# A two-layer conditioned transformer on one core: the first norm's scale and the first two projections of layer 0 interleaved by chunks of 128 features, with the loads in that order and three small inputs in one array

## The chip, the cores and the metric

The kernel runs on 1 core of one Trainium2 chip. The metric is the device time of one execution in microseconds (us). Kernel code is written per engine: TensorE (PE), VectorE (DVE), ScalarE (ACT), GpSimd (POOL) and SyncE (SP), which here only issues transfers. Each engine runs its own list of instructions in order; engines wait for each other and for transfers through semaphores.

## The reference, cut to what matters

x is (32, 64, 512): 32 entries of 64 tokens, 2048 tokens in all. cond_2048 is (32, 512), one row of conditioning for each entry.

```python
def ada_rms(x, t, w, tw):
    n = x * jax.lax.rsqrt(jnp.mean(jnp.square(x), axis=-1, keepdims=True) + EPS)
    scale = t @ tw.T
    return n * (w * (1.0 + scale))[:, None, :]
...
# layer 0: 8 query heads of 64, one key and one value head
h = ada_rms(x, time_emb, ln1_w, ln1_tw)
q, k, v = h @ Wq.T, h @ Wk.T, h @ Wv.T          # reshaped to heads
q, k = apply_rope(q, pos_ids), apply_rope(k, pos_ids)
attn = softmax(q k^T / sqrt(64)); x = x + (attn v) @ Wo.T
h = ada_rms(x, time_emb, ln2_w, ln2_tw)
x = x + (silu(h @ Wg.T) * (h @ Wu.T)) @ Wd.T     # inner size 2048
# layer 1: layernorm with scale and shift t @ W_ada.T + b_ada, latent keys and values,
# 16 query heads of 32, rope, softmax under a mask, output projection, residual
```

## The kernel before

The tokens are cut into 16 tiles of 128 (NT = 16; P = 128), so a tile holds two entries. Features are cut into four chunks of 128 (KT = 4). Layer 0's attention runs tile by tile, its MLP in blocks of 512 tokens, layer 1's attention tile by tile again; the MLP's matmuls are laid between the attention pieces of later tiles by numbers written out by hand (`FILL0`, `FILL1`). The order on each engine is the order of the code. This study concerns the first 30 us, in which nothing of the MLP is there yet.

**The scale of the first norm.** `condt` holds the conditioning turned (features on partitions, NB = 32 entries along the columns). For each chunk k of the contraction, `condition(k, ...)` issues four matmuls, one for each group g of 128 output features. The stationary operand is the same 128x32 piece of `condt`; each goes to a column tile of the array of its own (`tile_position=(0, NB * g)`) and so to its own 32 partitions of the bank BU. When all four chunks have been added up, ACT copies the 128x128 result to `tq` (`condition_copy`), PE turns it (`condition_T`), DVE forms (1 + scale) * w for all 512 features at once (`adaptive_scale(0, ...)`, L1255), and `scale_h(t)` multiplies the turned tile `xt[t]` of x by it (L1294, 128x512).

**The first two projections.** Tiles 0 and 1 are projected in full fp32: `first_qkv(t)` (L783) runs for each chunk k two matmuls of 320 columns (`QK0`; queries, keys and values are 640), with `xt[t][:, k]` stationary and `wst[:, k]` moving. Tile 2 and later ones use weights split into a high and a low part (`wqh`, `wql`): ACT rounds `wst[:, k]` to `wqh` (`split_qkv`, L1793), DVE subtracts it (`split_qkv`, L1262, 128x640, both inputs in SBUF). A tile is split in the same way: `high_h` on ACT, `low_h` on POOL (L563).

**After a projection.** `rope_mul(t)` on DVE (L1344, twice 128x640 out of PSUM, then two small ones for the keys, L1353 and L1354), `rope_sum(t)` on POOL (L574, L575), `qk_T(t)` on PE (L816, L817, five transposes), `keys(t)` on DVE (L1359) and `queries(t)` on ACT, then `scores(t)` on PE (L834). The rms factor of a tile comes from `square(t)` on ACT, `mean_sq(t)` on DVE and `rstd(t)` on POOL (L544, L552) and is folded into the rope tables `cs0`, for which `rope_mul(t)` waits. DVE also computes the angles of the rope (L1219 to L1248) at the start.

**Warming.** `keep_warm(n)` (L775) issues n matmuls of zeros with 256 columns into a bank that nobody reads.

**Loads.** SP issues them in the order in which they are written: `condt`, four chunks of `adaw0` (the weights of the first scale, ln1_tw turned, cut along the contraction), `xt[0]`, four chunks of `wst`, then `xres[0]`, `xt[1]` and the rest. ACT issues the small ones (`posi`, `invt`, `idn`, `lnw` twice).

## Time and profile before

| | us |
|---|---|
| median of 3 runs | 836.48 (835.95 to 837.05) |
| the profiled execution | 836.44 |
| its span in the trace | 834.6 |
| PE busy | 827.2 (99%) |
| DVE busy | 598.5 (72%) |
| ACT busy | 414.1 (50%) |
| POOL busy | 392.4 (47%) |

The span runs from the first to the last instruction in the trace; the 1.8 us more of the execution's own time lie around it. A busy PE is one that has an instruction in flight: matmuls overlap, and a record's length holds the way through the array as well. An fp32 matmul that is not a transpose leaves two records. Every time in the rows below counts from the start of the span.

### The profile page before, as it was taken

The page shows a single profiled execution, that of the slowest core. Times are in us where ns is not written, and L with a number is a line of the kernel's source. Part 1 is how long each engine was busy: PE and PEld are TensorE (multiplying, and loading weights), DVE is VectorE, ACT ScalarE, POOL GpSimd, SP SyncE. Part 2 cuts the span into 40 slices and gives each one's busy share as a digit, 9 for nine tenths or more (in the row PEclk, how much of TensorE's full clock was granted, in tenths as well). Part 3 has the DMA queues.
Part 4 walks back from the last instruction along what each step waited for, and adds up shares of the span by engine and source line. Part 5 has one row for each costly group of instructions (what it writes and reads, how often), then busy time and mean ns, then how long its engine had stood idle before and what let it go on. Part 6 is the DMA issues. An engine that isn't in the chain of part 4 may idle for free.

```text
span 834.6 us, 15041 instructions
## 1 busy us (share of the span) xinstructions
PE 827.2 (99%) x5688; PEld 678.6 (81%) x5688; DVE 598.5 (72%) x889; ACT 414.1 (50%) x725; POOL 392.4 (47%) x310
## 2 busy tenths in 40 slices
PE   9999999999999999999999999999999999999998
PEld 5888878888788788787888887888878878878886
DVE  6986567666665766766656878877867668678997
ACT  4555445435345344345446475373453543735662
POOL 2667535545544446446545755454443533532110
PEclk9999999999999999999999999999999999999999
DMA  9913442433523523424444445355254353330001
GB/s 334 387 34 110 137 158 98 162 119 116 175 101 104 183 92 131 158 68 154 145 154 143 144 166 196 115 177 169 83 184 155 105 196 124 124 132 14 15 27 52
DMA packets 73335, 113.50 MB, mean 136 GB/s; under 512 B 6320, under 2 KB 39088, under 8 KB 73264
## 3 DMA queue, kind: packets, MB, share of 16 engines
q1 hardware_dynamic: 72544, 112.45, 39.8%
q8 instruction: 46, 0.75, 0.4%
q14 instruction: 25, 0.20, 0.1%
q10 hardware_dynamic: 720, 0.09, 0.1%
HBM read 88.15 MB, written 24.38 MB: 135 GB/s over the span
## 4 chain that ended last, share of the span: by engine, by line
PE 95%; DVE 2%; DMA 1%; issue 1%; ACT 0%; POOL 0%; SPq 0%; ACTq 0%; DVEq 0%; POOLq 0%
PE ps L736 29%; PE ps L738 28%; PE ps L737 28%; PE ps L1024 2%; PE ps L834 1%; PE ps L1052 1%; PE ps L783 1%; DMA pT<-turned_p 1%; PE ps L864 1%; PE ps L775 1%; DVE ex L1529 1%; PE ps L1032 1%; PE ps L745 1%; PE ps L992 0%; DMA turned_p<-tp 0%
## 5 line engine op out<-in xcount | busy, mean ns | idle before, releaser
L736 PE MATMUL ps<-h2h,guh 128*128 128x512 f32 x512 | 203.5, 397 | 0.0
L738 PE MATMUL ps<-h2l,guh 128*128 128x512 f32 x512 | 199.9, 391 | 0.0
L737 PE MATMUL ps<-h2h,gul 128*128 128x512 f32 x512 | 199.3, 389 | 0.0
L590 POOL TENSOR_TENSOR gul<-rgu,guh 128x1024 fp32r<-128x1024 f32 x64 | 161.0, 2516 | 71.2 <-ACT guh L1890 71.2
L595 POOL TENSOR_TENSOR wdl<-rwd,wdh 128x512 fp32r<-128x512 f32 x64 | 83.5, 1304 | 129.4 <-ACT wdh L1898 129.4
L1415 DVE TENSOR_TENSOR xres<-ps,xres 128x512 f32<-128x512 f32 x128 | 87.4, 684 | 62.7 <-PE ps L738 62.7
L736 PEld LDWEIGHTS ps<-h2h,guh 128*128 128x128 f32 x512 | 96.0, 188 | 27.4 <-issue 7.7
L738 PEld LDWEIGHTS ps<-h2l,guh 128*128 128x128 f32 x512 | 96.1, 188 | 21.2
L737 PEld LDWEIGHTS ps<-h2h,gul 128*128 128x128 f32 x512 | 96.2, 188 | 19.1
L736 PE MATMUL ps<-wdh,ah 128*128 128x512 f32 x256 | 100.1, 391 | 0.0
L737 PE MATMUL ps<-wdh,al 128*128 128x512 f32 x256 | 99.6, 389 | 0.0
L738 PE MATMUL ps<-wdl,ah 128*128 128x512 f32 x256 | 99.6, 389 | 0.0
L1898 ACT CAST wdh<-rwd 128x512 fp32r<-128x512 f32 x64 | 39.4, 616 | 107.5 <-PE ps L738 104.3
L1410 DVE TENSOR_TENSOR al<-af,ah 128x512 fp32r<-128x512 f32 x64 | 64.7, 1011 | 36.8 <-ACT ah L1909 36.3
L1405 DVE TENSOR_TENSOR af<-ps,sg 128x512 f32<-128x512 f32 x64 | 44.0, 688 | 64.4 <-PE ps L738 46.6
L1909 ACT CAST ah<-af 128x512 fp32r<-128x512 f32 x64 | 39.6, 618 | 87.9 <-DVE af L1405 87.9
L1903 ACT ACTIVATE sg<-ps 128x512 f32<-128x512 f32 x64 | 38.2, 596 | 89.7 <-PE ps L738 89.5
L1890 ACT CAST guh<-rgu 128x1024 fp32r<-128x1024 f32 x64 | 67.0, 1046 | 0.0
L736 PEld LDWEIGHTS ps<-wdh,ah 128*128 128x128 f32 x256 | 48.0, 188 | 10.9 <-DVE al L1410 1.0
L738 PEld LDWEIGHTS ps<-wdl,ah 128*128 128x128 f32 x256 | 48.0, 188 | 10.1
L737 PEld LDWEIGHTS ps<-wdh,al 128*128 128x128 f32 x256 | 48.1, 188 | 9.8
L627 POOL TENSOR_TENSOR yl<-yf,yh 128x512 fp32r<-128x512 f32 x16 | 20.6, 1290 | 56.4 <-ACT yh L1988 56.4
(199 smaller groups left out, 1588.1 us busy)
## 6 DMA issues: line engine op xcount, KB each, us to landing
rgu<-gu SPq DMA_DIRECT2D x64, 512.0 KB, 4.7
rwd<-WdT SPq DMA_DIRECT2D x64, 256.0 KB, 4.2
turned_q<-tq SPq DMA_DIRECT2D x20, 320.0 KB, 3.0
qkT<-turned_q SPq DMA_DIRECT2D x20, 320.0 KB, 3.2
turned_p<-tp SPq DMA_DIRECT2D x9, 512.0 KB, 2.6
pT<-turned_p SPq DMA_DIRECT2D x9, 512.0 KB, 4.0
xt<-xT SPq DMA_DIRECT2D x15, 256.0 KB, 2.9
out<-xres SPq DMA_DIRECT2D x15, 256.0 KB, 3.5
```

Of the source, the lines that this page charges most:

```text
L590: pool.tensor_tensor(gul[i][:, :], rgu[i][:, :], guh[i][:, :], ALU.subtract).then_inc(m_gul, 1)
L595: pool.tensor_tensor(wdl[r][:, :], rwd[n % 2][:, :], wdh[r][:, :], ALU.subtract).then_inc(m_wdl, 1)
L736: pe.matmul(dst, lh, rh, start=start, stop=False)
L737: pe.matmul(dst, ll, rh, start=False, stop=False)
L738: return pe.matmul(dst, lh, rl, start=False, stop=stop)
L1405: dve.tensor_tensor(af[:, :], bank(BU), sg[:, :], ALU.mult).then_inc(m_af, 1)
L1410: dve.tensor_tensor(al[n % RING][:, :], af[:, :], ah[n % RING][:, :], ALU.subtract).then_inc(m_al, 1)
L1415: dve.tensor_tensor(at, bank(down_bank(q, i)), at, ALU.add).then_inc(m_x, 1)
L1890: act.copy(guh[i][:, :], rgu[i][:, :]).then_inc(m_guh, 1)
L1898: act.copy(wdh[r][:, :], rwd[n % 2][:, :]).then_inc(m_wdh, 1)
L1903: act.activation(sg[:, :], bank(BG), ACT.Silu).then_inc(m_sg, 1)
L1909: act.copy(ah[n % RING][:, :], af[:, :]).then_inc(m_ah, 1)
```

## The change

Four things are changed together.

1. **The first scale goes by groups of output features.** `first_scale(g)` computes the scale of the 128 features of group g completely: four matmuls, one for each chunk k of the contraction, all four to the same column tile (0, NB * g). ACT copies 32x128 of it (`first_scale_copy`), `first_scale_T(g)` turns it, DVE's `first_scale(g)` forms (1 + scale) * w for that group and `scale_part(t, g)` multiplies that chunk of `xt[t]` (128x128). For this, ln1_tw comes from the host in another layout, so that a chunk of `adaw0` holds one group of outputs with the whole contraction.
2. **The projections of tiles 0 and 1 are cut by chunk**, `first_qkv(t, k)`, and laid between the pieces of the scale. The transposes of tile 0 come after both, with half of the second norm's scale (`condition_second`) ahead of them and half behind. One `keep_warm(1)` stands between the first scale's matmuls and its transpose; the three between the chunks are gone.
3. **The loads follow**: `condt`, then `adaw0` chunk, `wst` chunk, and so on, with both `xt` ahead; the loads of `adaw1`, `adaw2` and `xres[3:6]` are cut into pieces with semaphores of their own.
4. **The identity, the two norm weights and the inverse frequencies come in one array** `small` (tile `consts`, 128x168), in one transfer in place of four; `condT` comes with 512 contiguous bytes to a partition.

DVE, ACT and POOL have their early work in another order, too: on DVE, angle steps, `first_scale`, `scale_part` and `split_qkv` are interleaved, and on POOL `rope_sum(0)` comes ahead of `low_h(2)`.

The diff, cut to its core (POOL's part is word for word the three lines of its reordering):

```diff
-            sp.dma_start(condt[:, :, :], by_row(condT)).then_inc(ld_cond, 16)
-            for k in range(KT):
-                sp.dma_start(adaw0[:, k, :], by_row(ln1_twT)[:, k, :]).then_inc(ld_ln1[k], 16)
-            load_xT(0)
-            for k in range(KT):
-                sp.dma_start(wst[:, k, :], by_row(WqkvT)[:, k, :]).then_inc(ld_qkv[k], 16)
-            sp.dma_start(xres[:, 0, :], xv[:, 0, :]).then_inc(ld_x0, 16)
-            load_xT(1)
+            sp.dma_start(condt[:, :, :], condT).then_inc(ld_cond, 16)
+            for g in range(KT):
+                sp.dma_start(adaw0[:, g, :], ln1_tw[g, :, :]).then_inc(ld_ln1[g], 16)
+                if g == 0:
+                    load_xT(0)
+                if g == KT - 1:
+                    sp.dma_start(xres[:, 0, :], xv[:, 0, :]).then_inc(ld_x0, 16)
+                sp.dma_start(wst[:, g, :], by_row(WqkvT)[:, g, :]).then_inc(ld_qkv[g], 16)
+                if g == 0:
+                    load_xT(1)
             sp.dma_start(xres[:, 1, :], xv[:, 1, :]).then_inc(ld_x1, 16)
             sp.dma_start(gf[:, :, :], xT[2, :, :, :]).then_inc(ld_x2t, 16)
-            sp.dma_start(adaw1[:, :, :], by_row(ln2_twT)).then_inc(ld_ln2, 16)
+            for k in range(KT):
+                sp.dma_start(adaw1[:, k, :], by_row(ln2_twT)[:, k, :]).then_inc(ld_ln2[k], 16)
             sp.dma_start(xres[:, 2, :], xv[:, 2, :]).then_inc(ld_x2, 16)
             sp.dma_start(wost[:, :, :], by_row(WoT)).then_inc(ld_wo, 16)
-            sp.dma_start(adaw2[:, :, :], by_row(adaT)).then_inc(ld_ada, 16)
+            for i, ks in enumerate((slice(0, 1), slice(1, KT))):
+                sp.dma_start(adaw2[:, ks, :], by_row(adaT)[:, ks, :]).then_inc(ld_ada[i], 16)
+            sp.dma_start(xres[:, 3, :], xv[:, 3, :]).then_inc(ld_x3, 16)
             load_xT(3)
-            sp.dma_start(xres[:, 3:6, :], xv[:, 3:6, :]).then_inc(ld_x3, 16)
+            sp.dma_start(xres[:, 4:6, :], xv[:, 4:6, :]).then_inc(ld_x4, 16)
...
             rstd(1)
+            rope_sum(0)
             low_h(2)
-            rope_sum(0)
+            rope_sum(1)
             rstd(2)
-            rope_sum(1)
...
+            def first_scale(g):
+                pe.wait_ge(ld_ln1[g], 16)
+                rows = slice(NB * g, NB * (g + 1))
+                for k in range(KT):
+                    mm = pe.matmul(ps[rows, first_bank(g), 0:P], condt[:, k, :], adaw0[:, g, P * k:P * (k + 1)],
+                                   start=(k == 0), stop=(k == KT - 1), tile_position=(0, NB * g))
+                mm.then_inc(first_mm, 1)
+
+            def first_scale_T(g):
+                pe.wait_ge(first_sb, g + 1)
+                rows = slice(NB * g, NB * (g + 1))
+                pe.transpose(ps[:, first_bank(g), P:P + NB], tq[rows, 0:P], idn[rows, rows],
+                             tile_position=(NB * g, 0)).then_inc(first_T, 1)
...
+            def first_qkv(t, k, between=None):
+
+                pe.wait_ge(a_xs[t], k + 1)
+                pe.wait_ge(ld_qkv[k], 16)
+                for c in range(2):
+                    mm = pe.matmul(ps[:, qkv_banks(t)[c], 0:QK0], xt[t][:, k, :],
+                                   wst[:, k, QK0 * c:QK0 * (c + 1)],
+                                   start=(k == 0), stop=(k == KT - 1))
+                    if c == 0 and between is not None:
+                        between()
+                if k == KT - 1:
+                    mm.then_inc(a_qkv, 1)
...
             pe.wait_ge(ld_cond, 16)
-            for k in range(KT):
-                pe.wait_ge(ld_ln1[k], 16)
-                mm = condition(k, in_blocks(adaw0, k))
-                if k < KT - 1:
-                    keep_warm(1)
-            mm.then_inc(ada_mm, 1)
-            pe.wait_ge(ld_idn, 16)
-            condition_T(1, 1, BD[0])
+            first_scale(0)
+            keep_warm(1)
+            pe.wait_ge(ld_const, 16)
+            first_scale_T(0)
             keep_warm(3)
-            first_qkv(0)
-            first_qkv(1)
+            first_qkv(0, 0)
+            first_scale(1)
+            first_qkv(1, 0, lambda: first_scale_T(1))
+            first_scale(2)
+            first_qkv(0, 1)
+            first_scale_T(2)
+            first_scale(3)
+            first_qkv(1, 1)
+            first_scale_T(3)
+            first_qkv(0, 2)
+            first_qkv(0, 3)
+            first_qkv(1, 2)
+            first_qkv(1, 3)
+            condition_second((0, 1))
             qk_T(0)
-            condition_second()
+            condition_second((2, 3))
             scores(0)
-            condition_T(2, 1, BG)
+            condition_T(1, 1, BG)
...
+            def first_scale(g):
+                dve.wait_ge(first_T, g + 1)
+                dve.scalar_tensor_tensor(out=sc_ln1[:, g, :], in0=ps[:, first_bank(g), P:P + NB], scalar=1.0,
+                                         in1=lnw[:, 0, g:g + 1].broadcast_to([P, NB]),
+                                         op0=ALU.add, op1=ALU.mult).then_inc(first_done, 1)
+
+            def scale_part(t, k):
+                dve.wait_ge(first_done, k + 1)
+                if k == 0:
+                    dve.wait_ge(ld_xt[t], 16)
+                h = xt[t][:, k, :].rearrange("p (b s) -> p b s", b=2)
+                dve.tensor_tensor(h, h, sc_ln1[:, k, 2 * t:2 * t + 2].unsqueeze(2).broadcast_to([P, 2, S]),
+                                  ALU.mult).then_inc(a_xs[t], 1)
+
...
-            adaptive_scale(0, sc_ln1, BD[0])
-            scale_h(0)
-            angles_end()
+            first_scale(2)
+            scale_part(0, 2)
+            scale_part(1, 2)
             split_qkv(0)
+            first_scale(3)
+            scale_part(0, 3)
+            mean_sq(0)
+            scale_part(1, 3)
             split_qkv(1)
-            mean_sq(0)
-            scale_h(1)
+            scale_h(2)
+            mean_sq(1)
+            rope_mul(0)
             split_qkv(2)
-            mean_sq(1)
-            scale_h(2)
-            rope_mul(0)
             split_qkv(3)
-            mean_sq(2)
             keys(0)
             rope_mul(1, lambda: softmax_sub(0))
+            mean_sq(2)
...
+            def first_scale_copy(g):
+                act.wait_ge(first_mm, g + 1)
+                rows = slice(NB * g, NB * (g + 1))
+                act.copy(tq[rows, 0:P], ps[rows, first_bank(g), 0:P]).then_inc(first_sb, 1)
...
-            condition_copy(1, 1)
+            first_scale_copy(0)
             split_qkv(0)
+            first_scale_copy(1)
+            split_qkv(1)
+            first_scale_copy(2)
+            split_qkv(2)
             rope_table(0)
-            split_qkv(1)
+            first_scale_copy(3)
             rope_table(1)
             square(0)
-            split_qkv(2)
             split_qkv(3)
             square(1)
             high_h(2)
-            square(2)
             values(0)
             act.activation(spare_exp[:, :], minus_half[:, :], ACT.Exp)
             queries(0)
-            condition_copy(2, 1)
+            condition_copy(1, 1)
+            square(2)
```

What moves on PE, at the start of the program. Before:

```order
L775 MATMUL ps<-zeros 128x256 x4
L745 MATMUL ps<-adaw,condt 32x128 x4
L775 MATMUL ps<-zeros 128x256
L745 MATMUL ps<-adaw,condt 32x128 x4
L775 MATMUL ps<-zeros 128x256
L745 MATMUL ps<-adaw,condt 32x128 x4
L775 MATMUL ps<-zeros 128x256
L745 MATMUL ps<-adaw,condt 32x128 x4
L755 MATMUL ps<-idn,tq 128x128
L775 MATMUL ps<-zeros 128x256 x3
L783 MATMUL ps<-wst,xt 128x320 x16
L816 MATMUL ps<-idn,qr 128x128 x4
```

And in the changed kernel (L804 is `keep_warm`, L770 `first_scale`, L777 `first_scale_T`, L811 `first_qkv`):

```order
L804 MATMUL ps<-zeros 128x256
L777 MATMUL ps<-consts,tq 128x32
L804 MATMUL ps<-zeros 128x256 x3
L811 MATMUL ps<-wst,xt 128x320 x2
L770 MATMUL ps<-adaw,condt 32x128 x4
L811 MATMUL ps<-wst,xt 128x320
L777 MATMUL ps<-consts,tq 128x32
L811 MATMUL ps<-wst,xt 128x320
L770 MATMUL ps<-adaw,condt 32x128 x4
L811 MATMUL ps<-wst,xt 128x320 x2
```

The 16 matmuls of the two projections stood in one piece behind the whole scale; now the first of them stand behind one quarter of it, and three quarters of the scale and three small transposes stand among them. The last eight of the 16 (chunks 2 and 3 of tile 0, then of tile 1) are in one piece again.

What moves on DVE, from the last scaling to the keys of tile 0. Before:

```order
L1262 TENSOR_TENSOR wql<-wst,wqh 128x640
L1280 TENSOR_SCALAR stat<-stat 128x1
L1294 TENSOR_TENSOR gf<-gf,sc_ln 128x512
L1344 TENSOR_TENSOR t<-ps,cs 128x640 x2
L1353 TENSOR_TENSOR qr<-t 128x2x32
L1354 TENSOR_TENSOR qr<-t 128x2x32
L1262 TENSOR_TENSOR wql<-wst,wqh 128x640
```

And in the changed kernel (L1321 is `split_qkv`, L1353 `scale_h`, L1403 to L1413 `rope_mul`, L1418 `keys`):

```order
L1321 TENSOR_TENSOR wql<-wst,wqh 128x640
L1353 TENSOR_TENSOR gf<-gf,sc_ln 128x512
L1339 TENSOR_SCALAR stat<-stat 128x1
L1403 TENSOR_TENSOR t<-ps,cs 128x640 x2
L1412 TENSOR_TENSOR qr<-t 128x2x32
L1413 TENSOR_TENSOR qr<-t 128x2x32
L1321 TENSOR_TENSOR wql<-wst,wqh 128x640 x2
L1418 COPY qkT<-ps 128x4x32
```

Between the rope of tile 0 and its keys stands one more of the four splits of the weights than before.

What moves on POOL, around the rope of tile 0. Before:

```order
L552 TENSOR_TENSOR cs<-cs,stat 128x64
L563 TENSOR_TENSOR hl<-gf,hh 128x512
L574 TENSOR_TENSOR qr<-t 128x8x32
L575 TENSOR_TENSOR qr<-t 128x8x32
L544 TENSOR_TENSOR stat<-stat,minus_half 128x1
```

And in the changed kernel (L588 and L589 are `rope_sum`, L577 `low_h`):

```order
L566 TENSOR_TENSOR cs<-cs,stat 128x64
L588 TENSOR_TENSOR qr<-t 128x8x32
L589 TENSOR_TENSOR qr<-t 128x8x32
L577 TENSOR_TENSOR hl<-gf,hh 128x512
L588 TENSOR_TENSOR qr<-t 128x8x32
```

The low part of tile 2 went from ahead of the rope of tile 0 to behind it.

## Rows read from the trace of the kernel before

**Rows 1.** The page: busy time of PE, and the chain that ended last.

```profile
PE 827.2 (99%) x5688; PEld 678.6 (81%) x5688; DVE 598.5 (72%) x889; ACT 414.1 (50%) x725; POOL 392.4 (47%) x310
...
PE 95%; DVE 2%; DMA 1%; issue 1%; ACT 0%; POOL 0%; SPq 0%; ACTq 0%; DVEq 0%; POOLq 0%
```

**Rows 2.** The chain in order of time: start us, us, what.

```profile
1.10 3.78 PE ps L775 x8
4.88 0.59 PE ps L745 x8
...
8.22 0.63 PE ps L775 x2
...
9.28 0.28 ACT tq L1798
...
9.99 1.30 PE ps L775 x6
11.29 8.77 PE ps L783 x32
20.05 0.62 PE ps L816 x4
...
20.78 1.01 PE ps L745 x32
21.79 0.62 PE ps L834 x32
22.41 0.26 PE ps L755
...
24.44 0.58 PE ps L816 x4
```

**Rows 3.** Timeline of DVE: start us, us, line, operation, tiles.

```profile
10.10 0.29 DVE L1255 SCALAR_TENSOR_TENSOR sc_ln<-ps,lnw 128x128 f32<-128x128 f32 x1 [1.24 <-PE ps L755]
...
12.56 1.55 DVE L1262 TENSOR_TENSOR wql<-wst,wqh 128x640 fp32r<-128x640 f32 x2
...
18.59 0.76 DVE L1354 TENSOR_TENSOR qr<-t 128x64 f32<-128x64 f32 x1
19.28 1.36 DVE L1262 TENSOR_TENSOR wql<-wst,wqh 128x640 fp32r<-128x640 f32 x1
...
20.82 0.29 DVE L1359 COPY qkT<-ps 128x128 f32<-128x128 f32 x1
21.02 1.55 DVE L1344 TENSOR_TENSOR t<-ps,cs 128x640 f32<-128x640 f32 x2
...
24.08 0.21 DVE L1354 TENSOR_TENSOR qr<-t 128x64 f32<-128x64 f32 x1
```

**Rows 4.** Timeline of POOL: start us, us, line, operation, tiles.

```profile
17.31 1.28 POOL L563 TENSOR_TENSOR hl<-gf,hh 128x512 fp32r<-128x512 f32 x1
18.54 0.74 POOL L574 TENSOR_TENSOR qr<-t 128x256 f32<-128x256 f32 x1
19.23 0.73 POOL L575 TENSOR_TENSOR qr<-t 128x256 f32<-128x256 f32 x1
...
22.65 0.74 POOL L574 TENSOR_TENSOR qr<-t 128x256 f32<-128x256 f32 x1 [0.94 <-DVE t L1344]
```

**Rows 5.** Stretches: us, busy of each engine, granted clock, DMA share, GB/s.

```profile
0.00:5.00 5.00, 3.90 (x12) 2.71 (x16) 0.14 (x1) 1.49 (x2) 0.55 (x6) 1.00 0.57 155
5.00:10.00 5.00, 4.52 (x40) 2.00 (x35) 3.66 (x7) 0.72 (x2) 0.00 (x0) 1.00 1.05 381
```

**Rows 6.** DMA issues (KB, us to landing) and the issue queues' timeline.

```profile
idn<-ident ACTq DMA_DIRECT2D x1, 64.0 KB, 4.1
wost<-WoT SPq DMA_DIRECT2D x1, 1024.0 KB, 11.4
...
8.78 0.46 SPq L459 DMA_DIRECT2D wost<-WoT  x1
```

More of the change, by code:

```diff
@@ L46, in fill, with build @@
         next(pieces, None)
-def build(nc, x, xT, pos, condT, ln1_w, ln1_twT, ln2_w, ln2_twT, WqkvT, WoT, gu, WdT,
-          adaT, b_ada, Wq1T, Wkd, wkvuT, Wo1T, invf, rope1, ident, out):
+def build(nc, x, xT, pos, condT, ln1_tw, ln2_twT, WqkvT, WoT, gu, WdT,
+          adaT, b_ada, Wq1T, Wkd, wkvuT, Wo1T, rope1, small, out):
     D = WoT.shape[0]
@@ L152, in build @@
             posi, posf = sb("posi", [P, NT], I32, l0), sb("posf", [P, NT], into=l0)
-            invt = sb("invt", [P, HD0 // 2], into=l0)
             sq = sb("sq", [P, D], into=l0)
@@ L165, in build @@
         smx1 = sb("smx1", [P, 3, 4 * KT])
-        (ld_pos, ld_cond, ld_lnw, ld_bada, ld_x0, ld_x1, ld_x2, ld_x2t, ld_idn, ld_wo, ld_x3, ld_x6, ld_ln2, ld_ada, ld_rope1,
-         ld_w1) = [sem("ld_" + n) for n in "pos cond lnw bada x0 x1 x2 x2t idn wo x3 x6 ln2 ada rope1 w1".split()]
+        (ld_pos, ld_cond, ld_const, ld_bada, ld_x0, ld_x1, ld_x2, ld_x2t, ld_wo, ld_x3, ld_x4, ld_x6, ld_rope1,
+         ld_w1) = [sem("ld_" + n) for n in "pos cond const bada x0 x1 x2 x2t wo x3 x4 x6 rope1 w1".split()]
         ld_ln1 = [sem(f"ld_ln1_{m}") for m in range(KT)]
+        ld_ln2 = [sem(f"ld_ln2_{m}") for m in range(KT)]
+        ld_ada = [sem(f"ld_ada_{m}") for m in range(2)]
+        first_mm, first_sb, first_T, first_done = [sem("first_" + n) for n in "mm sb T done".split()]
+        a_xs = [sem(f"a_xs{i}") for i in range(2)]
         ld_qkv = [sem(f"ld_qkv{k}") for k in range(KT)]
@@ L775, in keep_warm @@
                     pe.matmul(ps[:, BD[1], 0:2 * P], zeros[:, 0:P], zeros[:, :], start=True, stop=True)
-            def first_qkv(t):
-                pe.wait_ge(a_hf, t + 1)
-                for k in range(KT):
-                    pe.wait_ge(ld_qkv[k], 16)
-                    for c in range(2):
-                        mm = pe.matmul(ps[:, qkv_banks(t)[c], 0:QK0], xt[t][:, k, :],
-                                       wst[:, k, QK0 * c:QK0 * (c + 1)],
-                                       start=(k == 0), stop=(k == KT - 1))
-                mm.then_inc(a_qkv, 1)
+            def first_qkv(t, k, between=None):
[7 more added lines that the diff above has]
+                        between()
+                if k == KT - 1:
+                    mm.then_inc(a_qkv, 1)
             def qkv(t, between=None):
@@ L804, in qkv @@
                     for k in range(KT):
+                        if t == 2 and c == 0:
+                            pe.wait_ge(w0l, k + 1)
                         mm = three(ps[:, XB[c], 0:QK0], hh[:, k, :], hl[:, k, :], wqh[:, k, cols],
@@ L1228, in _ @@
             dve.tensor_scalar(turns, angle, 1.0 / TWO_PI, ROUND, ALU.mult, ALU.add).then_inc(ang_step, 1)
+            first_scale(0)
+            scale_part(0, 0)
             dve.wait_ge(ang_step, 3)
@@ L1238, in _ @@
                 step += 1
[L1240 to L1248 removed]
+                if part == C1:
+                    scale_part(1, 0)
+                if part == C2:
+                    first_scale(1)
+                    scale_part(0, 1)
+                    scale_part(1, 1)
+            dve.wait_ge(ang_step, step)
+            dve.tensor_scalar(red, red, float(np.float32(3.1415925)), -float(np.float32(3.1415925)),
+                              ALU.min, ALU.max).then_inc(ang_ready, 1)
+            dve.wait_ge(ang_ready, 1)
+            dve.scalar_tensor_tensor(out=angle, in0=red, scalar=-1.0, in1=red, op0=ALU.mult,
+                                     op1=ALU.max).then_inc(ang_step, 1)
+            dve.wait_ge(ang_step, step + 1)
+            dve.tensor_scalar(angle, angle, -1.0, float(np.pi / 2), ALU.mult, ALU.add).then_inc(ang_ready, 1)
             def adaptive_scale(n, tab, from_bank):
[L1251 to L1253 removed]
+                dve.wait_ge(ada_T, n)
                 by_block = ps[:, from_bank, 0:P].rearrange("p (k b) -> p k b", k=KT)
@@ L2068, in _ @@
             square(3)
[L2069 removed]
+            condition_copy(2, 2)
             for s in range(1, NT):
@@ L2199 @@
         "pos": turn(np.asarray(pos_BxS).reshape(B * T // 128, 128)),
-        "condT": turn(cond_2048),
-        "ln1_w": column(L0_cond_ln1_w), "ln1_twT": turn(L0_cond_ln1_tw),
-        "ln2_w": column(L0_cond_ln2_w), "ln2_twT": turn(L0_cond_ln2_tw),
+        "condT": np.ascontiguousarray(np.asarray(cond_2048).reshape(-1, D // 128, 128).transpose(2, 1, 0)),
+        "ln1_tw": np.ascontiguousarray(groups(L0_cond_ln1_tw).reshape(D // 128, 128, -1)), "ln2_twT": turn(L0_cond_ln2_tw),
         "WqkvT": turn(wqkv), "WoT": turn(L0_cond_Wo),
@@ L2207 @@
         "wkvuT": turn(kvu.reshape(-1, kvu.shape[-1])), "Wo1T": turn(wo1),
-        "invf": np.ascontiguousarray(np.broadcast_to(invf, (128, hd0 // 2))),
         "rope1": np.ascontiguousarray(np.concatenate([rope1] * (128 // T), 0)),
-        "ident": np.eye(128, dtype=f32),
+        "small": np.concatenate([np.eye(128, dtype=f32), column(L0_cond_ln1_w), column(L0_cond_ln2_w),
+                                 np.broadcast_to(invf, (128, hd0 // 2))], 1),
     }
```

69 lines of the change are left out of this document (30 added, 39 removed).

## The prediction

> **What bounds the kernel now.** First the page: PE is busy for 827.2 us, 99% of the span, and the chain that ended last lies on PE for 95% [rows 1]. So PE's list is the clock of the kernel: what comes later on PE near the start pushes everything behind it by as much, and nothing later has spare time to give it back. Then the chain in order of time for the part that is changed [rows 2]. The reader is to see three stretches. From 4.88 to 11.29 the first scale is formed: PE's four small pieces of work have warming matmuls between them (one pair takes 0.63), ACT's copy takes 0.28, and from 9.99 to 11.29 there are zeros only, while DVE makes the factor (0.29) and scales the tile [rows 2, 3]. From 11.29 to 20.05 run the projections of tiles 0 and 1, 8.77 without a gap. From 20.05 PE goes on without a gap through tile 0's transposes, the second norm's scale and, at 21.79, the scores. The 6.4 us before the projections are what the change can win, and it can win only PE time that holds nothing but zeros.
>
> **Step 1, the projections start earlier.** The loads allow it. By 10.00 the trace has moved 5 x 155 + 5 x 381 = 2680 KB [rows 5]. The first projection needs `condt`, one chunk of `adaw0`, `xt[0]` and one chunk of `wst`, 0.9 MB, which passes at about 5.3; chunk 1 of both weights is complete at 1.8 MB, about 7.7, and wanted at about 11 and 12. No later load binds: bytes and rate stay the same. The small array is issued second on ACT's queue; the identity took 4.1 from its issue [rows 6], so it is there by about 5.5, before 7.2.
> PE: the four matmuls of `first_scale(0)` go to one column tile. A warming record of 256 columns takes 3.78 / 8 = 0.47 at first and 1.30 / 6 = 0.217 later [rows 2], so PE works at the lower of its two levels (1.2 and 2.4 GHz) at first although the row of the stretch prints 1.00 [rows 5]. A record of 128 columns is half of that, 0.22 and 0.108. Eight records: 4.88 + 8 x 0.22 = 6.65. ACT's copy (0.28 and 0.1 around it) and the warming matmul lie side by side to about 7.2, the small transpose and three warming matmuls (0.3 and 1.30) follow to **8.8**. DVE's two small operations (each under the 0.29 of the whole factor) lie beside them. The projections so start 2.5 earlier than at 11.29.
>
> **Step 2, three quarters of the scale now stand among them.** What do four matmuls of 128 columns cost in one column tile? Before, 16 of them, going round the four tiles, took 1.01 for 32 records [rows 2], 0.032 a record, against 0.108 for a record that has the array to itself. That is 0.25 for four at one end (if a chain in one tile overlapped as well), 8 x 0.108 = 0.87 at the other. I take 0.87: the ratio 0.108 / 0.032 is nearly the four tiles, so it is the tiles that ran side by side, and a chain that adds into one place in one tile has nothing beside it. To this comes the change between a narrow tile and the full array: 0.63 for the two warming records behind a narrow piece, where 0.43 is their bare time, so 0.2 a round. Three pieces: 3 x 1.07 = 3.2. Three small transposes, each 0.15 (a full one 0.26 with its neighbours' change): 0.45. The end of the projections: 8.8 + 8.77 + 3.2 + 0.45 = **21.2**, against 20.05, **1.15 later**. The early start is more than paid back.
> The Trainium skill, TensorEngine Tiling (Array Packing), Key Properties, says that changing the tiling mode drains the array. The 0.2 a round agrees that a change costs something; if each of the further changes cost a whole drain, the length of a record beyond its own 0.108, the sum would be up to 1 us larger, an estimate from that page's rule. TensorE: Matmul & The Clock Gate, Part 3 (Packing small matmuls), of the Trainium skill lets matmuls overlap when their tiles differ; no row here has a chain in one tile.
>
> **Step 3, tile 0's transposes lose their cover.** Before, tile 0's rope lay beside tile 1's projection and ended just as PE came free (POOL's second half ran 19.23 to 19.96, PE went on at 20.05) [rows 2, 4]. Now tile 0's last chunk ends four matmuls before the end, 21.2 - 4 x 0.548 = 19.0. DVE comes to the rope at about 19.3 (its factor, scalings and a split stand before it), takes 1.55, POOL starts 0.08 later (22.57 to 22.65) and takes 0.74 + 0.73 less 0.05 [rows 3, 4]: 22.35. So `qk_T(0)` starts at **22.35**, 2.3 later than before; the half of the second scale that now lies ahead of it (0.54) is work that it had to do anyway, and about 0.5 is PE waiting. `low_h(2)`, now behind, costs nothing there: its reader comes at 24.
>
> **Step 4, tile 0's keys.** PE could start the scores at 22.35 + 0.73 + 0.6 = 23.65. But `keys(0)` on DVE now stands behind two splits instead of one, and they meet POOL. A split takes 0.78 alone (1.55 for two at 12.56); at 19.28, beside POOL's sum, it took 1.36; the small rope operation took 0.76 beside POOL's sum and 0.21 with POOL quiet; both ended when POOL's operation had ended, plus their own time [rows 3, 4]. So a DVE operation with two inputs in SBUF waits for a POOL operation that runs. By this: the rope's small ones to 21.8, the first split behind POOL's second half, 22.35 + 0.7 = 23.1, then `low_h(2)` (1.28) takes its turn to 24.4, the second split to 25.1, keys to **25.4**. If POOL's long one comes behind both splits instead, keys are there at 24.0. The scores so start at 24.0 to 25.4 against 21.79; I take 25.0, nearer to the end that the rows at 19.28 show: 3.2 later. The Trainium skill, SBUF — State Buffer, in its part on the shared port pair, states the same hold for both directions, the later one blocking fully; by it POOL's `low_h` could also be the one held, which is the end at 24.0.
>
> **Step 5.** Tile 1's rope starts behind `keys(0)`, so 1.55, 0.08 and 1.42 later `qk_T(1)` can start at 28.4, when PE, 2.65 behind the start of the scores as before (21.79 to 24.44) [rows 2], comes at 27.7 to 28.1; before there was no such wait. 0.1 to 0.5, I take 0.2. SP's four more issues (0.46 each) delay none that matters: `wost` landed 11.4 after its issue at 8.78, being behind others' bytes and not its own issue [rows 6].
>
> **The sum**: 3.2 + 0.2 = **3.4 us later**. The profiled execution, 836.44, stands 0.04 under the median of 836.48, so the same sum holds for it: **839.8**. The likeliest case's own range is +1.7 to +4.6.
>
> **The rivals.**
> *Not slower: a chain in one tile costs what the round of four did.* Then step 2 costs 3 x 0.45 and `first_scale(0)` 0.6, the projections end at 8.2 + 8.77 + 1.35 + 0.45 = 18.8, `qk_T(0)` starts at 19.9 and the scores at 21.3 to 22.8, -0.5 to +1.1: **836.8**. For it speaks 0.032 a record in the row of 32; against it that this row has four tiles. It decides where a piece costs under 0.45 instead of 1.07. 20%, all of it within 0.2%.
> *Faster:* that case, and the waits behind it shrink too, since more is ready in advance. The 0.2% (1.7 us, about what a measurement of this kernel tells from no change) must come from PE's gaps before 35 us. 834.6. No row names such a gap as one that the change removes: 9%.
> *Slower by more:* each of the changes of tile drains the array and both splits wait in turn: 1 more in step 2 and 0.4 more in step 4, **841.3**. It decides where a round costs 0.4 instead of 0.2. 9%.
> *The change does not do what it says:* a chunk lands late and the projections wait for it. By step 1 there are 3 us to spare at chunk 1; inside the 62% of my forecast.
>
> **How the numbers follow.** Forecast 62%, slower by more 9%: 71% slower by over 0.2%. 20% within, 9% faster. The range takes in most of the "not slower" case and "slower by more": 836.3 to 841.6; it leaves out the 9% below, some 6% of the 20%, and some 4% above.
>
> **What would show it.** Right: the first projection starts near 8.8; the eight records of a `first_scale` amid the projections lie 0.11 apart; the projections end near 21.2; PE waits at `qk_T(0)` for POOL's sum and at `scores(0)` for DVE's keys; from there every line of PE stands 3 to 4 later to the end. Wrong: records 0.03 apart and an end before 20; or splits of 0.8 beside POOL's `low_h`, keys at 24, and a shift of 2 or less; or a late shift that shrinks after 30, which would say that PE's list has room behind the start.

## The result and the profile after

The changed kernel takes **841.69 us** in the median of 5 runs (841.14 to 842.86) against 836.48 (835.92 to 837.06) in 5 runs of the kernel before beside it: ratio 1.0066, 95% interval 1.0054 to 1.0077, 5.2 us slower. The forecast was 839.8 with a range to 841.6. The direction and most places were right, the size was 1.8 too small and the time lies just outside the range. The profiled execution took 841.43.

The page of the changed kernel answers to [rows 1]:

```profile
PE 831.5 (99%) x5687; PEld 682.2 (81%) x5687; DVE 602.2 (72%) x898; ACT 415.4 (49%) x728; POOL 392.3 (47%) x310
PE 89%; DVE 4%; DMA 3%; issue 2%; ACT 2%; POOL 1%; SPq 0%; DVEq 0%; ACTq 0%; POOLq 0%
```

PE is still busy for 99%, but the chain that ended last has left it for 11% of the span instead of 5%. The timeline of PE in the changed kernel answers to [rows 2] (start us, us, engine, line, operation, tiles, count, and the idle time before with what ended it):

```profile
4.54 1.03 PE L770 MATMUL ps<-adaw,condt 128*32 128x128 f32 x8
...
7.70 1.24 PE L811 MATMUL ps<-wst,xt 128*128 128x320 f32 x4
8.87 1.06 PE L770 MATMUL ps<-adaw,condt 128*32 128x128 f32 x8
9.86 0.81 PE L811 MATMUL ps<-wst,xt 128*128 128x320 f32 x2
10.60 0.24 PE L777 MATMUL ps<-consts,tq 32*128 32x32 f32 x1
10.77 0.81 PE L811 MATMUL ps<-wst,xt 128*128 128x320 f32 x2
11.51 1.06 PE L770 MATMUL ps<-adaw,condt 128*32 128x128 f32 x8
12.50 1.34 PE L811 MATMUL ps<-wst,xt 128*128 128x320 f32 x4
13.78 0.24 PE L777 MATMUL ps<-consts,tq 32*128 32x32 f32 x1
...
14.94 1.34 PE L811 MATMUL ps<-wst,xt 128*128 128x320 f32 x4
16.21 0.24 PE L777 MATMUL ps<-consts,tq 32*128 32x32 f32 x1
16.39 4.58 PE L811 MATMUL ps<-wst,xt 128*128 128x320 f32 x16
20.89 0.64 PE L759 MATMUL ps<-adaw,condt 128*32 128x128 f32 x16
22.03 0.66 PE L847 MATMUL ps<-consts,qr 128*128 128x128 f32 x4 [0.50 <-POOL qr L589]
...
24.83 1.13 PE L865 MATMUL ps<-qkT 64*64 64x64 f32 x32 [1.46 <-DVE qkT L1418]
...
28.75 0.60 PE L847 MATMUL ps<-consts,qr 128*128 128x128 f32 x4
...
31.06 0.60 PE L874 MATMUL ps<-consts,ex 128*128 128x128 f32 x4
```

The same view of the kernel before puts its starts up to 0.12 earlier than the chain of [rows 2] does, and the comparisons below use it (first projection, `scores(0)`, tile 1's transposes, `p_T(0)`; the projections end at 20.02):

```profile
11.17 8.88 PE L783 MATMUL ps<-wst,xt 128*128 128x320 f32 x32
...
21.72 0.69 PE L834 MATMUL ps<-qkT 64*64 64x64 f32 x32
...
24.39 0.63 PE L816 MATMUL ps<-idn,qr 128*128 128x128 f32 x4
...
26.73 0.60 PE L843 MATMUL ps<-idn,ex 128*128 128x128 f32 x4
```

The projections start at 7.70 (11.17 before) and end at 20.89 (20.02 before). A piece of scale takes 0.99 from its start to the next line's (8.87 to 9.86), a small transpose 0.17. Then PE waits 0.50 at tile 0's transposes and 1.46 at its scores. `p_T(0)`, the transposes of tile 0's probabilities (L874), is at 31.06; the first trace of the kernel before has it at 26.73, so the shift there is 4.3. It is 4.3 at `context(0)`, the product of tile 0's probabilities and values that follows, 4.1 at the last tile of layer 0 and 5.0 at the end.

DVE's timeline answers to [rows 3], POOL's to [rows 4]:

```profile
21.31 3.17 DVE L1321 TENSOR_TENSOR wql<-wst,wqh 128x640 fp32r<-128x640 f32 x2
24.40 0.28 DVE L1418 COPY qkT<-ps 128x128 f32<-128x128 f32 x1
...
29.12 1.61 DVE L1448 TENSOR_TENSOR ex<-ex,smx 128x512 f32<-128x512 f32 x1
```

```profile
21.94 1.86 POOL L577 TENSOR_TENSOR hl<-gf,hh 128x512 fp32r<-128x512 f32 x1
...
28.88 1.30 POOL L593 TENSOR_TENSOR wol<-wost,woh 128x512 fp32r<-128x512 f32 x1
```

Two splits ahead of tile 0's keys take 3.17 between POOL's sum and its low half for tile 2. And there is a second such place that the prediction did not name: `softmax_norm(0)` (L1448) takes 1.61 and ends 0.55 after `low_wo(0)` (L593, 28.88 to 30.18). In the kernel before `low_wo(0)` was nearly over when it began, and it took 0.69 (POOL's line, then DVE's):

```profile
24.37 1.29 POOL L579 TENSOR_TENSOR wol<-wost,woh 128x512 fp32r<-128x512 f32 x1 [0.29 <-DVE qr L1354]
...
25.56 0.69 DVE L1389 TENSOR_TENSOR ex<-ex,smx 128x512 f32<-128x512 f32 x1
```

The stretches of the changed kernel (columns as in [rows 5]) show loads at the same rate as before (377 GB/s from 5 to 10 us for 381), and a granted clock that fell:

```profile
20.00:25.00 5.00, 3.05 (x47) 1.85 (x49) 4.97 (x7) 3.89 (x8) 3.26 (x3) 0.96 1.02 399
25.00:30.00 5.00, 5.00 (x55) 4.87 (x55) 4.66 (x10) 2.70 (x5) 3.33 (x5) 0.70 1.06 378
```

Behind PE's two waits the granted clock was at its lower level (1.2 of 2.4 GHz) for 3.4 us; the scores took 1.13 (0.69 before). PE came to `p_T(0)` without a wait in this execution: its slow matmuls lay over the time in which the softmax was held.

### The profile page after: what moved, and what is told of

Its sections match the earlier page's. It is cut to its first block, busy times and chain, and to the rows that moved or that the text cites. A ratio compares the mean times of both kernels' runs of the same rounds, so it can differ in the third digit from the quotient of the medians.

```text
span 839.6 us, 15061 instructions
## 1 busy us (share of the span) xinstructions
PE 831.5 (99%) x5687; PEld 682.2 (81%) x5687; DVE 602.2 (72%) x898; ACT 415.4 (49%) x728; POOL 392.3 (47%) x310
## 4 chain that ended last, share of the span: by engine, by line
PE 89%; DVE 4%; DMA 3%; issue 2%; ACT 2%; POOL 1%; SPq 0%; DVEq 0%; ACTq 0%; POOLq 0%
PE ps L750 27%; PE ps L752 26%; PE ps L751 26%; PE ps L1055 1%; PE ps L865 1%; PE ps L1083 1%; PE ps L895 1%; DMA pT<-turned_p 1%; DVE ex L1588 1%; DMA turned_q<-tq 1%; PE ps L804 1%; POOL wol L662 1%; PE ps L1063 1%; PE ps L811 1%; PE ps L770 0%
```

## The experiments

Shifts below are against the first trace of the kernel before, where nothing else is said; every ratio is against runs of the kernel before on the same chip.

**Each kernel once more.** One trace of each was a thin basis, so both were profiled again, unchanged.

> The kernel before, unchanged, profiled once more. Theory (the shift that grows in layer 1 by 0.4 to 2.4 us between 455 and 720 us belongs to the single execution, not to the kernel): this second profile differs from the first by under 0.2 us to the end of layer 0 and by 0.5 to 1.5 us behind 455 us. Rival (the first profile is typical): under 0.3 us everywhere.

> The changed kernel, unchanged, profiled once more. Theory (the waits of 0.50 and 1.46 us on TensorE and the held splits recur; whether the clock falls behind them, and how long the low level lasts at the start, differs by execution): scores(0) again 3.0 to 3.6 us and context(0) 4.0 to 4.6 us later than in the kernel before's first profile, the first piece of scale between 1.0 and 1.9 us. Rival (the profiled execution was an odd one): context(0) late by 3.4 or less.

They took 836.14 and 842.60. The second trace of the kernel before, on PE:

```profile
10.33 8.88 PE L783 MATMUL ps<-wst,xt 128*128 128x320 f32 x32
...
20.97 0.69 PE L834 MATMUL ps<-qkT 64*64 64x64 f32 x32
...
25.98 0.60 PE L843 MATMUL ps<-idn,ex 128*128 128x128 f32 x4
```

The second trace of the changed kernel, on PE:

```profile
4.81 1.69 PE L770 MATMUL ps<-adaw,condt 128*32 128x128 f32 x8
...
8.64 1.24 PE L811 MATMUL ps<-wst,xt 128*128 128x320 f32 x4
...
25.76 0.69 PE L865 MATMUL ps<-qkT 64*64 64x64 f32 x32 [1.45 <-DVE qkT L1418]
...
28.91 0.63 PE L847 MATMUL ps<-consts,qr 128*128 128x128 f32 x4 [0.42 <-POOL qr L589]
...
31.73 0.66 PE L874 MATMUL ps<-consts,ex 128*128 128x128 f32 x4 [0.33 <-DVE ex L1448]
```

The projections end, with the next line of PE, at 19.27 in the one and 21.83 in the other. The same work at the start takes a different time in each execution: the first piece of scale 1.03 or 1.69 in the changed kernel, 0.66 or 0.43 in the one before, and the first projection is up to 0.94 earlier or later. The first trace of the kernel before had a slow start, that of the changed kernel a quick one, so the two that stood side by side understate the shift. Like beside like:

| | both quick | both slow | predicted |
|---|---|---|---|
| projections end | 20.89 - 19.27 = 1.6 | 21.83 - 20.02 = 1.8 | 1.15 |
| scores(0) | 24.83 - 20.97 = 3.9 | 25.76 - 21.72 = 4.0 | 3.2 |
| p_T(0) | 31.06 - 25.98 = 5.1 | 31.73 - 26.73 = 5.0 | 3.4 |
| the execution's time | 841.43 - 836.14 = 5.3 | 842.60 - 836.44 = 6.2 | 3.4 |

So by 31 us the pairs are 5.1 and 5.0 apart. At the last tile of layer 0 they are 4.6 and 5.1 apart, and layer 1 adds 0.7 and 1.1: nearly all of the median's 5.2 arises in the first 31 us, and what layer 1 adds is taken up with the next run. Two starts are not two kinds, though: in the runs below that begin with the same instructions as the changed kernel, the first projection starts at 7.75 to 9.16. What the pairing can't settle is counted from the first projection on, in a table behind the runs.

The expectation that the two traces of the kernel before would agree to 0.2 until layer 1 fell (they differ by 0.5 from `context(0)` on); of the changed kernel scores(0) was 4.0 and context(0) 5.1 late, outside both expectations, for the same reason. The waits of 0.50 and 1.45 recur; the fall of the clock does not (1.00 in both stretches, scores 0.69).

**The array of small inputs alone** (`small_only`): the kernel before with one array for identity, norm weights and frequencies, and the turned `condT`.

> The kernel before with part 4 alone: the identity, norm weights and inverse frequencies in one array and one transfer, and condT with 512 contiguous bytes to a partition. Theory (these loads were in time anyway; PE waited for the weights of the scale): 836.4, between 0.3 us less and no change. Rival (the small loads or condt held the start): 0.5 to 1 us under the kernel before.

836.38 (836.22 to 837.75, 11 runs), ratio 1.0009 [1.0000, 1.0018]: nothing of the 5.2. Its profiled execution, one of 837.75, is level with the kernel before to 0.3 until 455 us and then 1.3 late, without any change of the code there. The changed kernel's two traces grow later by 0.9 and 1.1 behind the end of layer 0, the second trace of the kernel before by 0.2. Small waits for the turned queries or probabilities stand in layer 1 in all of them (0.2 to 0.6 each). `small_only` shows that such a growth needs no change in the work of the start, and that it weighs little in a median; its cause is open. Whether part of it belongs to the change is open, too: the traces of the variants below all grow there, by 0.4 to 2.4. Part 3 of the change, the order of the loads, has no run of its own: that it costs nothing rests on PE's waits, none of which up to 31 us is for a load in either trace of the changed kernel.

**One split fewer ahead of the keys** (`one_split`):

```diff
             split_qkv(2)
-            split_qkv(3)
             keys(0)
+            split_qkv(3)
             rope_mul(1, lambda: softmax_sub(0))
```

> The changed kernel with one edit on DVE: keys(0) stands between split_qkv(2) and split_qkv(3), not behind both. Theory (DVE's list as a whole is late behind tile 0's rope, because each split waits for a POOL operation): scores(0) start at about 23.5 instead of 24.83, but the split and rope_mul(1) behind it come no earlier, so the wait moves to qk_T(1), at about 27.8 instead of 28.75; about 1.0 us under the changed kernel, 840.7. Rival (the wait of scores(0) for keys(0) and the slow clock behind it are the whole loss, and nothing else on DVE is urgent): 2.6 us under it, 839.1, and no wait at qk_T(1).

841.68, ratio 1.0068 [1.0055, 1.0081]: no gain. PE's timeline:

```profile
23.54 0.69 PE L865 MATMUL ps<-qkT 64*64 64x64 f32 x32
...
27.80 0.63 PE L847 MATMUL ps<-consts,qr 128*128 128x128 f32 x4 [1.55 <-DVE qr L1413]
```

The scores are 1.3 earlier than in the changed kernel's first trace, the wait reappears at tile 1's transposes (1.55), and `p_T(0)` comes at 30.62. On DVE the two splits take 1.36 and 1.43, one on either side of the keys, and the softmax still takes 1.58. What binds there is not the keys alone but DVE's list up to the softmax: the split has only been moved within it.

**No idle PE, so that the clock stays up** (`warm_wait`): one and three matmuls of zeros in the two waits.

```diff
             condition_second((0, 1))
+            keep_warm(1, BG)
             qk_T(0)
             condition_second((2, 3))
+            keep_warm(3, BG)
             scores(0)
```

> The changed kernel with four more warming matmuls (zeros) into a bank that is free there: one ahead of qk_T(0), three ahead of scores(0), where PE waits 0.5 and 1.46 us. Theory (the waits themselves cost 3.0 us by the scores; 1.25 us more is lost because the clock stands at 0.5 for 3.4 us behind them): the granted clock is 1.00 in 25 to 30, scores(0) take 0.64 instead of 1.13, the first half of qkv(2) 1.85 instead of 2.45; 1.2 us under the changed kernel, 840.5. Rival (the matmuls behind the wait are slow for another cause, such as operands that come late): the same lengths and the same time, 841.7, or more by what the zeros overhang.

841.88, ratio 1.0068 [1.0056, 1.0081]. The clock is 1.00 throughout and the scores take 0.69, as the theory said, and still nothing is gained. PE waits 0.42 for POOL at tile 1's transposes, and DVE still holds the softmax up:

```profile
31.35 0.66 PE L874 MATMUL ps<-consts,ex 128*128 128x128 f32 x4 [0.33 <-DVE ex L1450]
```

The 3.4 us at the lower level lay beside a chain over DVE and POOL that was nearly as long: from the scores to `p_T(0)` it is 6.0 here and in the repeated trace, 6.2 where the clock fell. The clock is worth up to 0.3 in the one execution and nothing in the others.

**Four column tiles for a piece of scale** (`four_tiles`): the four matmuls go side by side, and a matmul with four identities on top of each other sums and turns.

```diff
             for k in range(KT):
+                rows = slice(NB * k, NB * (k + 1))
                 mm = pe.matmul(ps[rows, first_bank(g), 0:P], condt[:, k, :], adaw0[:, g, P * k:P * (k + 1)],
-                               start=(k == 0), stop=(k == KT - 1), tile_position=(0, NB * g))
+                               start=True, stop=True, tile_position=(0, NB * k))
```

> The changed kernel, but the four matmuls of a first_scale(g) go to four column tiles, one for each chunk of the contraction, without adding up in PSUM; the sum over the four is made by the turning matmul, whose moving operand is four 32x32 identities stacked (16 KB more to load), and the copy is 128x128 instead of 32x128. Theory (a chain in one tile has the array to itself for 0.108 a record): the eight records start 0.03 apart, a piece costs 0.4 instead of 0.99, the projections end near 18.6 instead of 20.9, everything behind comes 2.2 us earlier, the waits of qk_T(0) and scores(0) stay; 839.5. Rival (the piece is dear because of the change between tiled and full array, not because of the chain): at most 0.4 us are saved, 841.3.

839.59 (839.15 to 839.64), ratio 1.0040 [1.0026, 1.0053]: 1.8 of the 5.2 are gone. PE's timeline:

```profile
9.12 0.43 PE L772 MATMUL ps<-adaw,condt 128*32 128x128 f32 x8
9.48 0.81 PE L812 MATMUL ps<-wst,xt 128*128 128x320 f32 x2
...
18.91 0.64 PE L761 MATMUL ps<-adaw,condt 128*32 128x128 f32 x16
...
23.04 0.69 PE L866 MATMUL ps<-qkT 64*64 64x64 f32 x32 [1.45 <-DVE qkT L1420]
```

A piece costs 0.36 instead of 0.99. It is the chain in one tile that made it dear, as step 2 said; whether by the one tile or by adding up in one place is not told apart, since this run gives up both. But the projections end at 18.91, 1.1 before the first trace of the kernel before (20.02), and the scores still start 1.3 after: the waits behind are worth more than all that is done to PE's list.

**The splits and the statistics at their old places** (`early_split`, then `early_stats`, which has both). A split goes into DVE's gap of 0.98 before the last chunk's factor; then `square(2)`, `mean_sq(2)` and `rstd(2)` go back ahead of tile 0's values, keys and tile 1's sum.

```diff
             split_qkv(0)
+            split_qkv(1)
             first_scale(3)
...
-            split_qkv(2)
             split_qkv(3)
+            mean_sq(2)
             keys(0)
             rope_mul(1, lambda: softmax_sub(0))
-            mean_sq(2)
             softmax_norm(0)
```

> The changed kernel with one piece of DVE's work moved: split_qkv(1) stands right behind split_qkv(0), where DVE waits 0.98 us for the transpose of group 3, split_qkv(2) takes its place, and only split_qkv(3) stands between rope_mul(0) and keys(0). Theory (DVE's list, lengthened by twelve small operations and idle while PE forms the scale, is what PE waits for from 22 us on, with each split held by POOL's operation): keys(0) at about 22.9, scores(0) at 23.5, qk_T(1) at about 26.3 with no wait of more than 0.3; the start of context(0) 1.3 to 1.7 us under the changed kernel, and so its time, 840.2. Rival (as in the run one_split, something behind the keys binds, for one the factor of the softmax held by POOL's low_wo): scores(0) early but context(0) no earlier than 0.4 us, 841.3.

> early_split, and besides the statistics of tile 2 (square(2), mean_sq(2), rstd(2)) in the places that they had in the kernel before, ahead of keys(0) and of rope_sum(1). Theory (moved behind, they push low_wo(0) on POOL into DVE's last operation of softmax_norm(0), which took 1.61 instead of 0.69): low_wo(0) ends before or at the start of that operation, it takes 0.7, context(0) starts 0.4 to 0.9 us earlier than in early_split; 839.6. Rival (that hold is covered by PE's own work): no difference from early_split.

840.30, ratio 1.0052 [1.0040, 1.0065], and 840.19, ratio 1.0044 [1.0032, 1.0057]. DVE's timeline of the second:

```profile
28.78 0.69 DVE L1448 TENSOR_TENSOR ex<-ex,smx 128x512 f32<-128x512 f32 x1
```

The hold of 0.92 is gone (0.69 for 1.61). PE's lines at tile 1's transposes and `p_T(0)` show what it was worth, first in `early_split`, then in `early_stats`:

```profile
27.89 0.63 PE L847 MATMUL ps<-consts,qr 128*128 128x128 f32 x4 [0.24 <-issue]
...
30.71 0.65 PE L874 MATMUL ps<-consts,ex 128*128 128x128 f32 x4 [0.32 <-DVE ex L1448]
```

```profile
27.63 0.63 PE L847 MATMUL ps<-consts,qr 128*128 128x128 f32 x4 [0.23 <-issue]
...
29.97 0.60 PE L874 MATMUL ps<-consts,ex 128*128 128x128 f32 x4
```

From the one to the other it is 2.82 with the hold, as in the second trace of the changed kernel (28.91 to 31.73), and 2.34 without it, as in the kernel before (24.39 to 26.73). So 0.48 of the 0.92 reaches PE. `context(0)` is 4.0 late with the split alone and 3.2 with both, but 0.25 of that is the start (first projection at 9.16 and 8.91). The medians tell the two apart by 0.1 only, so alone the statistics' place is shown in the trace, not in the time; and the interval of either ratio overlaps that of the changed kernel (1.0054 to 1.0077). The profiled execution of `early_split` is the slowest of its five, 842.85, by what layer 1 adds.

**Both repairs together** (`four_early_stats`):

> four_tiles together with the orders of early_stats (here split_qkv(1) and split_qkv(2) both stand behind the last scalings and ahead of scale_h(2)). Theory (the three causes add up: narrow chains 1.8, splits 1.3, statistics 0.4): context(0) 0.6 to 1.1 us behind the kernel before, 837.2. Rival (they cover one another, so that the sum is less than the parts): 838.5 or more.

837.29 (836.96 to 838.93, 11 runs), ratio 1.0016 [1.0007, 1.0025]. With four tiles in place the old order is worth 2.3 us. The softmax takes 0.69, the scores start at 22.00. PE's timeline:

```profile
20.55 0.66 PE L848 MATMUL ps<-consts,qr 128*128 128x128 f32 x4 [1.19 <-POOL qr L591]
```

What is left of the loss, 1.1 in the median and 0.5 at `context(0)`, begins with 1.19 of waiting at tile 0's transposes, which have no projection of another tile beside tile 0's rope any more.

**Splits on POOL** (`four_pool_splits`): the last kernel, with splits 0 to 2 on POOL, which was idle.

> four_early_stats, but three of the four splits of wqk (0, 1, 2) are made by POOL, which is idle until 15, instead of DVE. Theory (what is left of the loss is DVE's list): context(0) within 0.3 us of the kernel before, 836.4 plus what the waits for transfers in layer 1 add, at most 837.0. Rival (POOL's long operations, 1.6 us each, hold DVE's small scalings on which PE waits): waits of PE before the projections' pieces, 838 or more.

838.71, ratio 1.0032 [1.0019, 1.0044], worse by 1.4. POOL's timeline, then DVE's:

```profile
9.98 1.55 POOL L669 TENSOR_TENSOR wql<-wst,wqh 128x640 fp32r<-128x640 f32 x1 [1.50 <-ACT wqh L1855]
12.24 1.68 POOL L669 TENSOR_TENSOR wql<-wst,wqh 128x640 fp32r<-128x640 f32 x1 [0.71 <-ACT wqh L1855]
```

```profile
10.49 1.39 DVE L1274 TENSOR_TENSOR xt<-xt,sc_ln 128x128 f32<-128x128 f32 x2
...
12.52 1.69 DVE L1309 TENSOR_SCALAR ex<-ex 128x512 f32<-128x512 f32 x1
```

Two scalings take 1.39 instead of 0.49, a tensor_scalar 1.69 instead of 0.43; PE waits 0.34 to 0.53 for the scaled chunks at three places.

**Tile 0's rope first** (`four_rope_first`): the kernel with both repairs, and scaling tile 2 behind the rope (on ACT, `high_h(2)` goes behind `values(0)` and the table load, ahead of `queries(0)`).

```diff
             split_qkv(2)
-            scale_h(2)
             mean_sq(1)
             rope_mul(0)
+            scale_h(2)
             split_qkv(3)
```

> The kernel with four column tiles, early splits and early statistics, and besides tile 0's rope on VectorE ahead of scaling tile 2 (0.78), whose cast on ScalarE follows behind the table load. Theory (what is left of the loss, +0.6 at context(0), is tile 0's transposes without cover: they wait 1.19 for GpSimd's sum, which follows the rope): the rope starts at about 16.9 instead of 17.45, the transposes at 19.95 instead of 20.55 with a wait of 0.6, keys at 20.8, the scores at 21.3 to 21.4 instead of 22.0, 0.4 ahead of the kernel before; context(0) 0.1 after to 0.3 ahead of before's; the whole 836.6. Rival (GpSimd's low half for tile 2, now later, holds PE at tile 2's projection or VectorE's operations): scores as above, but context(0) stays 0.6 late or more, the whole 837.3 to 837.8.

837.84 (837.32 to 838.96, 11 runs) against 836.78 here, ratio 1.0013 [1.0003, 1.0022]. PE's timeline:

```profile
19.78 0.66 PE L848 MATMUL ps<-consts,qr 128*128 128x128 f32 x4 [0.79 <-POOL qr L591]
...
21.47 0.69 PE L866 MATMUL ps<-qkT 64*64 64x64 f32 x32 [0.34 <-ACT qkT L1911]
...
24.87 0.63 PE L848 MATMUL ps<-consts,qr 128*128 128x128 f32 x4 [0.48 <-POOL qr L591]
```

Tile 0's scores are 0.5 earlier than in `four_early_stats`, but 0.36 of that is the start (first projection at 7.40 for 7.76): 0.2 is won, and 0.34 of waiting for ACT's queries, behind the cast moved there, is new. Tile 1's transposes are where they were (24.94 there), and so 0.3 later counted from the start: POOL's low half and statistics of tile 2 stand ahead of its sum. The rival comes nearest, with 837.84 for its 837.3 to 837.8; `context(0)` is 0.5 late. POOL's and DVE's lists bind, and moving one piece pays at one tile what it costs at the next. No order tried beats the kernel before.

**All runs, counted from the first projection.** This takes the start out. Starts are from PE's timelines.

| us | first projection at | to `scores(0)` | on to tile 1's transposes | on to `p_T(0)` | together |
|---|---|---|---|---|---|
| before | 11.17 | 10.55 | 2.67 | 2.34 | 15.56 |
| before, second trace | 10.33 | 10.64 | 2.67 | 2.34 | 15.65 |
| `small_only` | 11.11 | 10.52 | 2.68 | 2.34 | 15.54 |
| changed, where the clock fell | 7.70 | 17.13 | 3.92 | 2.31 | 23.36 |
| changed, second trace | 8.64 | 17.12 | 3.15 | 2.82 | 23.09 |
| `warm_wait` | 8.27 | 17.12 | 3.13 | 2.83 | 23.08 |
| `one_split` | 7.75 | 15.79 | 4.26 | 2.82 | 22.87 |
| `early_split` | 9.16 | 15.77 | 2.96 | 2.82 | 21.55 |
| `early_stats` | 8.91 | 15.78 | 2.94 | 2.34 | 21.06 |
| `four_tiles` | 7.95 | 15.09 | 3.13 | 2.84 | 21.06 |
| `four_early_stats` | 7.76 | 14.24 | 2.94 | 2.34 | 19.52 |
| `four_rope_first` | 7.40 | 14.07 | 3.40 | 2.34 | 19.81 |
| `four_pool_splits` | 7.35 | 15.56 | 2.94 | 2.34 | 20.84 |

Where the same work is done and the clock stays up, the traces agree to 0.1, though their starts are up to 0.8 apart within the kernel before and 0.9 within the changed one. Against the changed kernel's second trace the early split is worth 1.5, the statistics 0.5 and the four tiles 2.0; all three together are worth 3.6 and not 4.1, so they cover one another in a small part.

## Why the prediction was right, and where it was short

**Right: what the change does and the sign.** Only PE time with zeros in it is won, and more is paid back behind. The loads never bind (PE waits for none of them up to 31 us in the changed kernel's traces, and the rate is that of [rows 5]; the diff gives SP five more issues, not the four of step 5). The rival of a change that does not do what it says is out.

**Step 1** gave 8.8 for the first projection. It was 7.70 and 8.64, and up to 9.16 in the other runs. The first piece was priced from a slow start [rows 2]; the quick one takes 0.7 less than the slow one. Since the kernel before wins about as much by a quick start (10.33 for 11.17), this moves the difference little.

**Step 2 failed too, by 0.8.** From the first projection to the end it came to 12.4; both traces have 13.2. A piece costs 0.99 (1.07 with its change of tile was predicted, so 0.2 too much for three), a transpose 0.17 (0.15). What is missing is on the projections: the first 16 records, between narrow pieces, take 1.17 + 0.74 + 0.74 + 1.28 + 1.27 = 5.2 by their starts, the last 16, undisturbed, 4.50, so another 0.7 for the six narrow pieces and transposes among them. In `four_tiles`, where only three narrow pieces are left there, the same 16 records take 4.88 and the last 16 take 4.49: 0.4, and again 0.12 to 0.13 for a narrow piece. The rival "slower by more" had named these changes, with 1.0. The Trainium skill, TensorEngine Tiling (Array Packing), Key Properties, states that a change of tiling mode drains the array; the trace agrees, with 0.12 for each narrow piece beside its own time. The rival "not slower" rested on a piece under 0.45; `four_tiles` shows that price, 0.36, but for four tiles only.

**Step 3** gave 22.35 and a wait of 0.5: 22.03 with 0.50, and 22.97 with 0.50. The way from the projections' end to the transposes was right (1.15 predicted, 1.14 in both). That 22.03 is near 22.35, and in step 4 24.83 near 25.0, is partly luck: the quick start of that execution, 1.1 ahead of 8.8, hides the 0.8 that step 2 lacks.

**Step 4** gave 25.0 (24.0 to 25.4), the keys behind two splits that POOL holds: 24.83 and 25.76, 2.8 behind the transposes in both where 2.65 was predicted. The two splits took 3.17, and both ways of the hold occur: POOL's `low_h` took 1.86 instead of 1.28 as well.

**Step 5 is the step that failed most, at 0.2.** From the scores to `p_T(0)` the changed kernel takes 6.2 and 6.0, the kernel before 5.0 in both traces. The second trace, without the fall of the clock, shows where its 1.0 lies: 0.48 up to tile 1's transposes, with 0.42 of waiting for POOL's sum, and 0.48 from there to `p_T(0)`, with 0.33 of waiting for the softmax. The first half is a size: with keys and scores at 25.0 the step's own terms give 25.0 + 1.55 + 0.08 + 1.42 = 28.05 against PE's 27.65, 0.4, and 0.2 was taken. The second half is a term left at nothing. The step stopped at tile 1's transposes; behind them stands `softmax_norm(0)`, held 0.92 by `low_wo(0)`. That meeting was made by a part of the change that the prediction did not cost at all: `rstd(2)` and its two predecessors, moved behind tile 0's keys and tile 1's sum, push `low_wo(0)` from ahead of the softmax into it. `early_stats` undoes just this on top of `early_split`: the operation takes 0.69 again, and the 0.48 is gone. In the first trace PE does not wait there: the slow matmuls in front take the place of both waits, and 0.3 more.

**The sum.** Like beside like, the 1.15 at the projections' end was 1.6 to 1.8, the 3.2 at the scores 3.9 to 4.0, and the 0.2 behind was 1.0 to 1.2: 5.0 at 31 us for 3.4. The misses point the same way, a moved or inserted operation whose neighbours were not all counted; the 0.2 too much in the price of the pieces works against them.

## What to carry to other kernels

When small pieces are put among big matmuls, price three things: the chain itself (four matmuls into one column tile took 0.99, in four tiles 0.36), each change between narrow and full array (0.12 for a narrow piece here), and what the interleaving takes away as cover from the work that follows the first tile. When a statistic or any small operation moves, follow its queue until everything behind it has run once: an operation of POOL that drifts beside one of DVE with two inputs in SBUF can hold that one until it ends (0.92 here, of which 0.48 reached PE). And before a shift of 1 us is read off two profiles, count it from a piece of work that lies behind the start (here traces then agree to 0.1 instead of 0.9), and take a second profile of each.

## What the runs showed of the hardware

- The start is not the same in every execution, though the rows print a clock of 1.00: one and the same piece of eight records took 1.03, 1.32, 1.69, 1.80 and 1.92 (`after`, `warm_wait`, `after_again`, `early_stats`, `early_split`), and between the two traces of the changed kernel every line of PE from the first projection to `scores(0)` lies 0.9 apart by it.
- After waits of 0.50 and 1.46 us on PE, with small matmuls between, the granted clock fell to its lower level for 3.4 us in one execution and not in the other of the same kernel, with waits of 0.50 and 1.45. It cost up to 0.3 at `p_T(0)`.
- DVE and POOL hold each other beyond the operations that the prediction counted: a tensor_scalar with one input in SBUF took 1.69 instead of 0.43 beside POOL's split (`four_pool_splits`, 12.52 beside 12.24 to 13.92), while the rope's multiplication, which reads PSUM, took its usual 1.55 beside POOL's low half (`four_early_stats`, 21.56 to 23.11 beside 20.46 to 22.32). The Trainium skill, SBUF — State Buffer, in its part on the shared port pair, states a lock for the whole instruction between the two engines; the trace agrees, with 1.61 for 0.69 at the softmax, which ends 0.55 after POOL's operation.
